# One software-pipelined attention and FFN layer: the shift's DMA moves to SyncE, the norm chain to even slots, and both up products of a tile stand together

## The reference, cut to what matters

```python
x = x + xattn(layernorm(x), ctx)        # x: (64, 64, 256), ctx: (64, 64, 64)
x = x + ffn(layernorm(x), w1, w2)

def xattn(hq, kv_c, ...):               # 16 heads, head size 128
    q_hk  = (hq @ Wq.T).reshape(b, s, H, K)
    q_big = einsum('bshk,hkq->bshq', q_hk, w_kc_q)
    kv_rope = kv_c * cos + rotate_half(kv_c) * sin
    q_r = einsum('bshq,hqr->bhsr', q_big, W_qr)
    k_r = einsum('bld,hdr->bhlr', kv_rope, W_kr)
    attn = softmax(einsum('bhsr,bhlr->bhsl', q_r, k_r))
    ctx_c = einsum('bhsl,bld->bhsd', attn, kv_rope)
    ctx_lat = einsum('bhsd,hkd->bshk', ctx_c, w_kc_kv)
    return ctx_lat.reshape(b, s, H * K) @ Wo.T

def bitlinear158(x, w):                 # RMS norm, activations to 8 bits, weights to -1, 0, 1
    return einsum('bsd,od->bso', activation_quant(simple_rmsnorm(x)), weight_quant(w))

def ffn(x, w1, w2):                     # inner width 1024
    return bitlinear158(gelu(bitlinear158(x, w1)), w2)
```

## Time and profile before

| | |
|---|---|
| median of 3 runs | 535.19 us (532.72 to 535.34) |
| the profiled execution | 532.06 us |
| its span, first to last instruction | 530.3 us |
| mean granted TensorE clock | 0.953 of full speed |
| slot 0 starts | 65.72 us |
| slots 7 to 30 | 142.40 to 452.67 us |
| slots 21, 22 and 23 start | 324.44, 338.31, 350.17 us |
| slot 31 to the end | 452.67 to 530.26 us, 77.6 us |

### The profile page before, as it was taken

How to read it: one execution, slowest core, us unless ns; L and a number is a source line. 1 busy time by engine, 2 the same in 40 slices (tenths; PEclk the granted TensorE clock), 3 DMA queues, 4 the chain that set the end, 5 groups by cost and what they waited for, 6 DMA issues and landing times. The chain is left out here.

```text
span 530.3 us, 8880 instructions
## 1 busy us (share of the span) xinstructions
PE 422.4 (80%) x2823; PEld 297.3 (56%) x2823; DVE 365.7 (69%) x894; ACT 253.5 (48%) x464; POOL 220.5 (42%) x270
## 2 busy tenths in 40 slices
PE   3998767998788788989898989898889896763644
PEld 1498644766656365647575757575656663452422
DVE  0634127888777777777777777777786858875694
ACT  0111343433364646565747473746565656435430
POOL 0300200264335445545454545454636273755432
PEclk9999989999899899989999999999999899988875
DMA  8970901112122225242533434333334333425253
GB/s 245 377 259 0 355 4 42 42 43 82 37 57 52 62 49 93 53 101 59 94 72 82 75 79 82 71 79 75 82 70 83 72 81 72 101 52 114 64 100 80
DMA packets 62798, 48.96 MB, mean 92 GB/s; under 512 B 51168, under 2 KB 56288, under 8 KB 61728
## 3 DMA queue, kind: packets, MB, share of 16 engines
q1 hardware_dynamic: 60576, 48.13, 37.3%
q10 hardware_dynamic: 2176, 0.26, 0.3%
HBM read 32.11 MB, written 4.46 MB: 69 GB/s over the span
## 5 line engine op out<-in xcount | busy, mean ns | idle before, releaser
L468 POOL TENSOR_TENSOR cl<-cr,ch 128x512 fp32r<-128x512 f32 x64 | 80.4, 1278 | 193.4 <-ACT ch L549 193.4
L549 ACT ACTIVATE ch<-cr 128x512 fp32r<-128x512 f32 x64 | 37.1, 623 | 113.4 <-DVE cr L838 113.4
L708 PE MATMUL hps<-bh,ch 128*128 128x256 f32 x256 | 78.0, 305 | 11.0 <-issue 10.9
L659 PE MATMUL ps<-xh,ah 128*128 128x256 f32 x256 | 78.9, 308 | 1.7 <-DVE xl L800 1.4
L660 PE MATMUL ps<-xl,ah 128*128 128x256 f32 x256 | 73.8, 288 | 0.0
L661 PE MATMUL ps<-xh,al 128*128 128x256 f32 x256 | 73.5, 287 | 0.0
L709 PE MATMUL hps<-bl,ch 128*128 128x256 f32 x256 | 73.3, 286 | 0.0
L710 PE MATMUL hps<-bh,cl 128*128 128x256 f32 x256 | 73.2, 286 | 0.0
L815 DVE TRANSPOSE_TENSOR_REDUCE red<-pe 128x16 f32<-128x512 f32 x64 | 41.7, 690 | 44.5 <-ACT pe L544 44.5
L531 ACT ACTIVATE qf<-ps 128x512 f32<-128x512 f32 x64 | 37.7, 589 | 61.8 <-PE ps L661 61.8
L732 PE MATMUL ps<-w1q,xqt 128*128 128x512 bf16 x128 | 39.6, 398 | 30.3 <-ACT g L564 26.9
(11 more groups left out here) (115 smaller groups left out, 853.7 us busy)
## 6 DMA issues: line engine op xcount, KB each, us to landing
rb<-rinv_d SPq DMA_DIRECT2D x64, 256.0 KB, 3.9
xs<-x SPq DMA_DIRECT2D x4, 1024.0 KB, 20.8
out<-yo SPq DMA_DIRECT2D x32, 128.0 KB, 2.7
wq_s<-wq SPq DMA_DIRECT2D x1, 2048.0 KB, 17.8
wo_s<-wo_t SPq DMA_DIRECT2D x1, 2048.0 KB, 9.5
w_s<-w_t SPq DMA_DIRECT2D x2, 1024.0 KB, 12.8
rinv_d<-ri SPq DMA_DIRECT2D x128, 2.0 KB, 1.4
wk_a<-wk_t SPq DMA_DIRECT2D x2, 512.0 KB, 6.0
```

Of the source, the lines that this page charges most:

```text
L468: pool.tensor_tensor(cl[:, u % 2, :, b * S:(b + 1) * S], cr[:, :, b * S:(b + 1) * S], ch[:, u % 2, :, b * S:(b + 1) * S].bitcast(F32), ALU ...
L659: pe.matmul(o, ah[:, c, cols], xh[:, k % 2, c, :], start=(c == 0), stop=False)
L708: pe.matmul(O[:, 0:D], c_h, bh[:, hp, :], start=(hp == 0), stop=False)
```

## The change

Seven things move; what is computed stays.
- `shift_rows` is issued by SyncE in place of ScalarE. On SyncE it stands behind the transposes that are due early in the slot and ahead of `rinv_rows`; in odd slots one `turn_g` follows behind it. Both `turn_g` of a pair now stand in odd slots, both `turn_x` in the even slot before the one that they were in.
- `rinv_rows` issues two DMAs in place of four, and the DMA of `rinv_spread` reads its rows in another order.
- `norms` moves from the end of an odd slot (behind `row_sum`) to the start of the even slot after it (ahead of `row_max`). `row_sum` goes ahead of `divide`; `x_lo` and `x_scale` go behind `divide` and `residual`; both `g_max` and `g_scale` stand ahead of `quadrant_sum`.
- `x_round` goes to the start of an even slot on GpSimd; `norm_x` goes from its start to its end.
- `up` of an even slot does both halves of its tile, right behind `scores`. In an odd slot one half stands ahead of `shifts` and the other at the end; the third half is gone from there. `gelu` follows the same order.
- `square_x` and `square_g` go ahead of `ctx_hi` on ScalarE.
- `finish` stands in slot t+10 in place of t+11 and `store` in t+11, so that the loop has two slots less (`LAST`).

```diff
@@ -52,7 +52,7 @@
 GB = 4
-LAST = NT + 12
+LAST = NT + 10
 NORM_STEPS = RSQRT_OPS + 3
@@ -366,7 +366,7 @@
             if n % 2 == 0 and tile(n - 7):
-                USES.append(("h", n - 7, 1))
+                USES += [("h", n - 7, 0), ("h", n - 7, 1)]
             if k < NB:
@@ -376,7 +376,7 @@
             if n % 2 and tile(n - 7):
-                USES += [("h", n - 7, 0), ("h", n - 7, 1), ("h", n - 6, 0)]
+                USES += [("h", n - 7, 0), ("h", n - 7, 1)]
@@ -404,22 +404,29 @@
             def _(sp):
+                def shift_rows(u):
+                    p = u % 2
+                    sp.wait_ge(sem["row_maxima"], u + 1)
+                    at_least(sp, sem["shifted"], 2 * (u - 1))
+                    for gg in range(2):
+                        sp.dma_start(shift[BB * gg:BB * gg + 2, p, :].bitcast(F32).rearrange("b (k s) -> b k s", s=32),
+                                     nmax[:, p, 32 * gg:32 * gg + 32].bitcast(F32)).then_inc(sem[f"shift_rows{p}"], 16)
+
                 def rinv_rows(u):
...
                     at_least(sp, sem["rinv_spread"], 32 * (u - 1))
-                    for gg in range(2):
-                        for b in range(2):
-                            sp.dma_start(rinv_d[p, gg ^ b, b, :].rearrange("(k s) -> k s", s=32),
-                                         ri[64 + 16 * b:64 + 16 * b + 16, p, 32 * gg:32 * gg + 32]).then_inc(sem[f"rinv_stored{p}"], 16)
+                    for b in range(2):
+                        sp.dma_start(rinv_d[p, b, :, :].rearrange("g (k s) -> k g s", s=32),
+                                     ri[64 + 16 * b:64 + 16 * b + 16, p, :].rearrange("k (g s) -> k g s", s=32)).then_inc(sem[f"rinv_stored{p}"], 16)
...
                     p = u % 2
-                    sp.wait_ge(sem[f"rinv_stored{p}"], 64 * (u // 2 + 1))
+                    sp.wait_ge(sem[f"rinv_stored{p}"], 32 * (u // 2 + 1))
                     at_least(sp, sem["ctx_divided"], 2 * u)
                     for half in range(2):
-                        sp.dma_start(rb[64 * half:64 * half + 64, :, :].rearrange("p b n -> p (b n)"),
-                                     rinv_d[p, half, :, :].rearrange("b n -> (b n)").partition_broadcast(64)).then_inc(sem["rinv_spread"], 16)
+                        rows = rinv_d[p, :, :, :].rearrange("b g n -> (b g) n")[half:4 - half:3 - 2 * half, :]
+                        sp.dma_start(rb[64 * half:64 * half + 64, :, :], rows.partition_broadcast(64)).then_inc(sem["rinv_spread"], 16)
@@ -441,16 +448,20 @@
                 for n in range(LAST + 1):
-                    if n % 2 and tile(n - 7):
-                        turn_x(n - 7)
+                    if n % 2 == 0 and tile(n - 6):
                         turn_x(n - 6)
-                    if tile(n - 10):
+                        turn_x(n - 5)
+                    if n % 2 and tile(n - 10):
                         turn_g(n - 10)
-                    if tile(n - 12):
-                        store(n - 12)
+                    if tile(n):
+                        shift_rows(n)
+                    if n % 2 and tile(n - 9):
+                        turn_g(n - 9)
                     if tile(n - 1):
...
                         rinv_spread(n - 1)
+                    if tile(n - 11):
+                        store(n - 11)
                 sp.wait_ge(sem["out_stored0"], 16 * (NT // 2))
@@ -502,19 +513,21 @@
                 for n in range(LAST):
-                    if n % 2 == 0 and tile(n + 4):
-                        norm_x(n + 4)
-                        norm_x(n + 5)
-                    if tile(n - 9):
+                    if n % 2 == 0 and tile(n - 6):
+                        x_round(n - 6)
+                        x_round(n - 5)
+                    if n % 2 and tile(n - 9):
                         g_round(n - 9)
...
                         ctx_lo(n - 2, 1)
-                    if n % 2 == 0 and tile(n - 6):
-                        x_round(n - 6)
-                        x_round(n - 5)
                     if tile(n - 3):
                         centre(n - 3)
+                    if n % 2 == 0 and tile(n + 4):
+                        norm_x(n + 4)
+                        norm_x(n + 5)
+                    if n % 2 == 0 and tile(n - 9):
+                        g_round(n - 9)
                     if n in (3, 5):
@@ -580,14 +593,6 @@
-                def shift_rows(u):
@@ -598,6 +603,7 @@
                     if n % 2 == 0 and tile(n - 7):
+                        gelu(n - 7, 0)
                         gelu(n - 7, 1)
@@ -605,19 +611,17 @@
                         x_hi(k + 1)
-                    if tile(n):
-                        shift_rows(n)
                     if n == 0:
                         w_sum(1)
+                    if tile(n - 4):
+                        square_x(n - 4)
+                    if tile(n - 8):
+                        square_g(n - 8)
                     if tile(n - 2):
...
                         q_out(k, b + 1)
-                    if tile(n - 4):
-                        square_x(n - 4)
-                    if tile(n - 8):
-                        square_g(n - 8)
                     if tile(n):
@@ -630,7 +634,6 @@
                         gelu(n - 7, 1)
-                        gelu(n - 6, 0)
@@ -752,6 +755,7 @@
                     if n % 2 == 0 and tile(n - 7):
+                        up(n - 7, 0)
                         up(n - 7, 1)
@@ -781,8 +785,6 @@
                         kv_t((n + 2) // 4)
-                    if n % 2 and tile(n - 7):
-                        up(n - 7, 1)
                     if tile(n - 1):
@@ -791,7 +793,7 @@
                     if n % 2 and tile(n - 7):
-                        up(n - 6, 0)
+                        up(n - 7, 1)
@@ -827,7 +829,7 @@
                     dve.wait_ge(sem["rinv_steps"], 2 * u + 1)
-                    at_least(dve, sem[f"rinv_stored{u % 2}"], 64 * (u // 2))
+                    at_least(dve, sem[f"rinv_stored{u % 2}"], 32 * (u // 2))
                     dve.reciprocal(ri[hi, u % 2, :], rs[hi, u % 2, :]).then_inc(sem["rinv_steps"], 1)
@@ -922,44 +924,45 @@
                     k = n // 2 + 1
-                    if tile(n - 11):
-                        finish(n - 11)
                     if tile(n):
...
                         x_max(n - 4)
-                    if n % 2 and tile(n - 5):
-                        x_scale((n - 5) // 2)
-                    if n % 2 and k + 1 < NB:
-                        x_lo(k + 1)
-                    if n % 2 == 0 and tile(n - 8):
-                        g_max(n - 8)
+                    if n % 2 == 0 and 0 <= (n - 6) // 2 < NB + 2:
+                        norms((n - 6) // 2)
                     if tile(n):
                         row_max(n)
+                    if tile(n - 1):
+                        row_sum(n - 1)
                     if tile(n - 2):
...
                         divide(n - 2, 1)
+                    if n % 2 and k + 1 < NB:
+                        x_lo(k + 1)
                     if tile(n - 3):
                         residual(n - 3)
-                    if tile(n - 1):
-                        row_sum(n - 1)
+                    if n % 2 and tile(n - 5):
+                        x_scale((n - 5) // 2)
+                    if n % 2 == 0 and tile(n - 8):
+                        g_max(n - 8)
+                        g_max(n - 7)
+                        g_scale((n - 8) // 2)
+                        if tile(n - 10):
+                            finish(n - 10)
                     if n == 0:
                         w_means()
-                    if n % 2 and 0 <= (n - 5) // 2 < NB + 2:
-                        norms((n - 5) // 2)
                     if tile(n):
...
                         quadrant_sum(n, 1)
+                    if tile(n - 10) and (n % 2 or not tile(n - 8)):
+                        finish(n - 10)
                     if n == 0:
...
                         ternary(n - 1)
-                    if n % 2 == 0 and tile(n - 8):
-                        g_max(n - 7)
-                        g_scale((n - 8) // 2)
                     if 1 <= n < 9:
```

6 lines of the change are left out of this document (removed).

## The result

| | before | after |
|---|---|---|
| median of 4 runs each, us | 535.27 | 476.56 |
| lowest and highest, us | 532.72, 536.98 | 475.33, 477.9 |
| ratio, with its 95% interval | | 0.891 [0.886, 0.895] |
| span of the profiled execution, us | 530.3 | 474.8 |
| start of slot 0 | 65.72 | 66.35 |

The forecast was 494 us with a range from 481 to 513. The span is 55.5 us shorter: 38.6 of that in slots 7 to 30, 9.9 at the end, 4.3 in slots 0 to 5, 3.3 in slot 6, and 0.6 went back ahead of slot 0.

A forecast was written before the change was run, and what follows sets the result against it. The prediction took TensorE as fullest engine (422.4 of 530.3 us), with odd slots ScalarE's from the shift on. Its terms, slots 7 to 30, slot 0, slot 6 and the end: 532.06 - 26 - 3 - 3 - 6 = 494 us, range 481 to 513.

The forecast's parts named there:

- TensorE's floor: Slots 7 to 30: TensorE's own work in an odd plus an even slot, put at 22.5 us against 25.86 before.
- bound for this part, 40 us: Slots 7 to 30: gain if no new wait came at all, where 26 us was forecast; lower bound 2.
- New waits 1 and 2: TensorE: `up` waits for `x_lo` ahead of `shifts` in odd slots, 0.5 us; `queries` for `gelu` in even slots, 0.6.
- the 0.1 for the shift: Even slots: `shifts` expected 0.1 us late, at +8.6 us, behind `norms` and `row_max`.
- The 2.04 us behind `down`: Odd slots: TensorE's wait of 2.04 us for `gelu` before the third half of `up`, expected to go whole.
- `norms`: 2.7 us: VectorE, even slots: norm chain of 2.7 us in place of 4.9, just covered by TensorE's turn of the maxima.
- Slot 0 and slot 6: 3 us from the second weight sum in slot 0, 3 us from the turn of the maxima in slot 6.
- The end: After the slots: `project`'s waits for `finish`, 2.43 and 3.76 us, both go; 6 us won, bounds 0 and 12.
- Rival A: SyncE, odd slots: the shift queues behind the turnings, costing 10 us, time near 504; chance 0.14.
- Rival B: Even slots become VectorE's, a pair costs 1.2 us more, time near 508; chance 0.17.
- Rival C: SyncE, odd slots: waits for GpSimd's `g_round` with the shift behind it; slower, 545 us; chance 0.04.
- Rival D: Whole kernel: the waits found are only shadows of a longer chain, nothing is won, 532 us; chance 0.05.

The follow-up runs named there:

- e10: Kernel after, with `x_lo` right behind `row_max` and `project`'s first half ahead of `queries` in even slots: 471.3 us, ratio 0.878.
- e3: Kernel after, with the third half of `up` behind `shifts` and the fourth behind `down` again, with their `gelu`: 486.29 us, ratio 0.911.
- e1: Kernel after, with the shift issued by ScalarE again, between `x_hi` and the squares: 493.42 us, ratio 0.923.
- e4: Kernel after, with both squares behind `ctx_hi` and `q_out` on ScalarE again: 495.18 us, ratio 0.927.
- e6: Kernel before, with only the shift moved to SyncE, behind `store`: 515.18 us, ratio 0.961.
- e2: Kernel after, with `norms` at the end of odd slots again: 487.22 us, ratio 0.913.
- e7: Kernel before, with only `norms` moved to even slots, ahead of `row_max`: 539.32 us over all runs; ratio 0.991 from two of ten executions.
- e13: Kernel after, with `finish` one slot later at the head of VectorE's slot, its store left in place: 475.65 us, ratio 0.888.
- e11: Kernel after, with both `turn_g` of an odd slot ahead of the shift on SyncE: 492.93 us, ratio 0.922.
- e8: Kernel after, with `x_lo` right behind `row_max`, ahead of `row_sum` and `divide`: 475.39 us, ratio 0.887.

## Why the prediction was wrong

The direction held, and so did the mechanism in the slots; the size did not: 38 us forecast, 55.5 in the traces. Of the 17.5 us between, 12.6 lie in slots 7 to 30, 3.9 at the end and 1.6 in slots 0 to 6, and 0.6 ahead of slot 0 went the other way. The floor below is the largest single step, about 8 us; with it alone put right the forecast had been 486, within the range. It left the range because every other term was too small as well.

- **TensorE's floor, the step that failed: 22.5 for a pair, measured 21.8 to 21.9.** It was worked out as slot length minus the idle time in brackets. Slots 21 and 22 after, less their two waits, are 10.88 and 11.15, the latter with a `kv_t` worth 0.25 on average; 10.88 + 10.90 is 21.8; the mean pair of 22.77 less 0.89 of waits is 21.9; and e10 runs pairs at 22.04 with 0.4 of waiting left. The brackets count only from a matmul's modelled end, which lies beyond the start that the next could have had: 0.16 us behind `down` above. Some waits got no bracket at all. In slot 21 before, it took 1.91 us from the half `up` at 331.78 through `shifts` and the second half to `ctx` at 333.69 (the first two are in the earlier trace rows); without the second half, 0.53, that is 1.38, and the same way now takes 0.99 (302.54 to 303.53), so `shifts` had waited 0.39 unseen (they start 2.44 after their DMA was issued, the time that it needs in the earlier trace rows). Behind `down` in slot 22 `scores` started after 1.19, now after 0.97, 0.22 more. These three places have 0.77 us, where a pair's floor was 0.6 to 0.7 too high, 8 us in all (the waits of the kernel after hide a little in their turn). The prediction itself said that a matmul's end is modelled and then subtracted brackets all the same. Its own bound for this part, 40 us, still held the 38.6 measured, and so did its bounds for slot 6 and the end, but the range of the sum left out "the far ends of the bounds", and four terms erred to the same side.
- **New waits 1 and 2: 0.5 and 0.6, measured 0.45 and 0.44.** Right in place and cause, in the rows named beforehand. With the 0.1 for the shift, which cost nothing, that is 0.3 less in a pair. Over slots 7 to 30 they come to 5.0 + 4.5 = 9.5 us, as each occurs 11 times, where the forecast had 14.4: 4.9 us less.
- **The 2.04 us behind `down`: gone whole, as said.** In the kernel after that is the order of `up`: only e3 brings the wait back, at 0.59 us. The prediction put it down to the shift's issues and the squares as well. Put back one by one these cost 17 us (e1) and 19 us (e4), but in the even slot; the odd one stays at 11.3.
- **`norms`: 2.7 us, measured 2.72, and covered by 0.21.** The stretching is gone: the L195 operation took 1.06 beside a GpSimd operation and now 0.16 with GpSimd at rest. The Trainium skill, page SBUF — State Buffer, section Who interferes with whom, states that a VectorE instruction with two inputs in SBUF contends with a GpSimd instruction that reads SBUF, over a port pair that is an exclusive lock. The trace agrees: the L195 operation has two inputs in SBUF, the GpSimd one beside it, L489, reads `g` there, and both end at 337.28.
- **Slot 0 and slot 6: 3 and 3, measured 4.4 and 3.3.** Both right in kind, slot 0 beyond its bound of 3.5; e6 and e1 give slot 0 to the shift (8.84 against 13.1), e2 and e7 give slot 6 to the norms.
- **The end: 6, measured 9.9, and half of the cause was wrong.** The prediction was right that both waits of `project` are for `finish`. But it gave them to `finish` standing a slot later, and only the second to the norms too. e13 puts `finish` back a slot later without loss; e2 puts the norms back, with `finish` where the change has it, and has both waits again.
- **Rival A** did not cost its 10 us: e11's row has the shift 2.55 us on the way behind turnings as elsewhere, and only a slot like e8's 25 shows more. The sign that the prediction gave for it, `shifts` more than 2.5 us after `row_max`, was badly chosen: in slot 21 of the kernel after they start 3.2 us after its end, held back by the `up` that waits for `x_lo`. The Trainium skill's rule that each DMA engine takes a ring's descriptors in order (page DMA: Bandwidth & Descriptors, section Queues, rings and completion order) can't be told from e11's row either way, since its second turning, issued at 303.34, had landed 3.1 us later, 0.8 ahead of `shifts`. **Rival B** did not come: even slots are TensorE's. **Rival C** did not decide here, but is real: e11 has it at 16 us. **Rival D**, that nothing is won, is gone with the time.

The 38.6 us of slots 7 to 30 are then 26 forecast, about 8 for the floor and about 5 for the waits. The clock is no part of the floor's error, as slots 21 and 22 were granted 1.00 before and after. It is a small part of the gain, which nothing here takes apart: before, slots 14 and 28 were granted 0.86 and took 12.3 us, where the other even slots from 12 to 26 took 11.6 to 12.0, and slots 9, 10 and 30 were granted 0.95, 0.93 and 0.88. After, slots 8 to 30 have 1.00.

What stays open: where the 3.4 us of the end's 9.9 come from that are not the norms' (the chain of `down` for `qt`, with waits of 4.4, 3.6 and 4.0 us in the last tiles, is the largest that is left there), and why the shift's move gives 4.4 us in slot 0 where the wait that was seen is 2.98.
